# Rows kept on chip, plain stores instead of adding ones, and scatter-adds held back to the end of a graph-and-experts kernel

## The chip, the cores and the metric

One Trainium2 chip, of which the kernel uses one core. The metric is the device time in microseconds of one execution. Before the change it is 1616.14 us, the median of 3 runs (1612.79 to 1617.56).

## The reference, cut to what matters

There are 6250 nodes with 256 features. A graph layer comes first, then a feed-forward layer of 8 experts, of which each node uses its two best.

```python
x = x + _L0_gnn_ref(_layernorm(x), src, dst, W, b)      # 106250 edges, segment sums
x = x + _L0_ffn_ref(_layernorm(x)[None], Wr, br, ln_g, ln_b, W1, b1, W2, b2)[0]
# within _L0_ffn_ref, for each node (D = 256, H = 1024, E = 8, TOP_K = 2):
probs = softmax(xt @ Wr + br);  top_p, top_idx = top_k(probs, 2)
weights = top_p / top_p.sum(-1)
xe = xn[None] * ln_g[:, None] + ln_b[:, None]           # xn: layer norm of xt
h = gelu(einsum('end,edh->enh', xe, W1) + b1);  y = einsum('enh,ehd->end', h, W2) + b2
out = (weights[:, :, None] * sel).sum(axis=1)           # sel: y of the two chosen experts
```

So the output row of a node is its row after the graph layer (called its base row here) plus two weighted expert rows.

## The kernel before, in words

The nodes lie in 49 tiles of 128, one to a partition. `acc[:, t, :]` (called `row(t)`) holds tile t: first the sums of its edges' messages, then its base row, written by `hh` on VectorE (L1846). Tiles are taken in 10 chunks (`ENDS`); chunk 9 (`LAST`) is tiles 45 to 48. The edges' source rows are gathered by 768 indirect DMAs from GpSimd (`fetch`, L920) that run until 1288.7 us, with PE reducing them by matmuls. As soon as a chunk of tiles is complete, its nodes are normalised, routed (`r1` to `r9`) and scattered to the experts' areas in `xs` (step `xs`, L951, two DMAs a tile from GpSimd). Before the last chunk's scatter the unused places have to hold a blank row: eight stores from SP (`blanks`, L1124), for which the scatter waits (L949).

The experts work on blocks of 256 rows, the last eight (49 to 56) on blocks of 128: 57 in all. A block's rows and the two weight matrices are loaded (`ld`, `ld2`: L1150, L1157, L1165; the weights 1024 KB each, the rows 260 KB, the bias 128 KB), PE turns the rows (L1427), multiplies them up (L1443) and down (L1458), ACT and VectorE work between, and VectorE's `y` step (L1935) takes the result out of PSUM.

How results reach the output:
- Blocks 0 to 33 (chunks 0 to 7, tiles 0 to 40; `M0` = 34, `TG` = 41) are stored in `ys` by SP (`st`, L1113). After the last of these, tile t's two expert rows are fetched from `ys` by two indirect DMAs of GpSimd (step `cg`, L970) into a ring of 10 places (`NC`), and VectorE's step `cc` (L1948, L1949) weighs and sums them in `row(t)`.
- Blocks 34 to 56 are weighed on VectorE (`y`, L1941) and added to the rows of `out` in memory by scattering DMAs with an add (step `give`, L983): two for each of the blocks 34 to 48, one for each of 49 to 56, so 38 DMAs in 23 steps.
- The base rows of all tiles are written to `out` by SP (`nd2`, L1106) early on; therefore the sums of the tiles 0 to 40 are then *added* to `out` by four DMAs of GpSimd of 10, 10, 10 and 11 tiles (step `sums`, L992).

Two adding DMAs that touch the same row must not overlap. So the steps `give` and `sums` form one chain: each waits for the one before it to have landed (`wait_last`, L929). The first waits for the base stores. A block's `y` writes into a ring of 8 places (`NQ`), so `y` of block m waits for the `give` of block m - 8 (L1934), for blocks 45 to 56.

Each engine's instructions stand in one order that `plan()` writes beforehand, by its own costs and a simulated clock: `step_job` lets a `cg` go when GpSimd's clock is at most 2.5 us ahead and the last chunk has been sent (L376), gives it 2.5 us and counts its data there 2 us after (L429); `step_give` (L316) sends `sums` when its tiles' `cc` are placed, and `give` when its `y` is, with 5 us between any two. Steps of different kinds on one engine stand in the planned order, whatever comes late on the chip.

Of the kernel before, what the change touches and what calls it, by code (L numbers as in the profile page):

```python
# [74 lines left out]
NSUM = 4  # L75
# [76 lines left out]
def ends(g):  # L152

    c, a0, a1 = GROUPS[g]
    return c if a1 == CHUNKS[c][1] else None
# [33 lines left out]
def plan():  # L189

    order = []
    clock = {"PE": 0.0, "DVE": 0.0, "ACT": 0.0, "POOL": 0.0}
    s = {"now": 0.0, "bank": 0.0, "held": {}, "free": {}, "norms": -1, "nT": 0, "nW": 0, "hh": 0, "xr": 0, "placed": 0, "tabled": 0, "read": -1, "routed": -1, "loaded": 0, "asked": False, "given": 0, "base": 1e9, "late": 1e9, "summed": 0, "chain": 0.0,
         "pb": 0, "pe": 0, "pG": 0, "ps": 0, "pz": 0, "ph": 0, "po": 0, "pw": 0, "wj": 0, "zl": 0, "zat": 1e9}
    later, sent = [], {}

# [118 lines left out]

    def step_give():  # L316

        if max(s["chain"], s["base"]) > s["now"] or clock["POOL"] > s["now"] + 2.6 or LAST not in sent:
            return False
        if batches and batches[0][0] <= s["now"]:  # L320
            b = batches.popleft()[1]
            emit("sums", b, (("POOL", 1.3 * (SUMS[b][1] - SUMS[b][0])),), s["now"])
            s["summed"] += 1
        elif gives and (BLOCKS[gives[0]][0] < LAST or s["late"] <= s["now"]):
            emit("give", gives[0], (("POOL", 1.7 * GIVES[gives.popleft() - M0]),), s["now"])
            s["given"] += 1
        else:
            return False
        s["chain"] = clock["POOL"] + 5.0
        return True  # L330
# [32 lines left out]
    def step_job(front):  # L363
        while front and front[0].over():
            done = front.popleft()
            if done.chunk is not None:
                sends.append(Job(send_stages(done.chunk), done.at))
        for job in list(itertools.islice(front, 2 if front is jobs or front is sends else 1)):
            job.over()
            for chain in job.heads():  # L370
                if not chain.steps:
                    continue
                kind, arg, costs = chain.steps[0]
                if chain.at > s["now"] or not free(costs):
                    continue
                if kind == "cg" and (clock["POOL"] > s["now"] + 2.5 or LAST not in sent):  # L376
                    continue
                if kind in ("wa", "wc", "we", "nW", "lg", "r3") and s["bank"] > s["now"]:
                    continue
                if kind in PARTS and (PARTS[kind][0] in s["held"] or s["free"].get(PARTS[kind][0], 0.0) > s["now"]):  # L380
                    continue
                if kind in ("nT", "xT") and len(turns) >= 2 and turns[-2] not in used:
                    continue
                if kind == "hh" and s["norms"] < group_of(arg):
                    continue
                if kind == "r1" and arg != s["placed"] or kind == "r5" and arg != s["tabled"] or kind == "r6" and arg - 1 != s["routed"]:
                    continue
                if kind in ("nT", "nW", "xr") and arg != s[kind]:
                    continue
                if kind == "nd2" and s["hh"] < GROUPS[arg][2]:  # L390
                    continue
                if kind in AFTER_STEP and s[AFTER_STEP[kind]] < arg:
                    continue
                if kind == "lg" and s["read"] < group_of(arg) - 1:
                    continue
                if kind == "xr" and PREV[GROUPS[arg][0]] is not None and sent.get(PREV[GROUPS[arg][0]], 1e9) > s["now"]:
                    continue
                chain.steps.popleft()
                end = emit(kind, arg, costs, s["now"])
                if kind in PARTS:  # L400
                    s["held"][PARTS[kind][0]] = PARTS[kind][1]
                for part in [p for p, k in s["held"].items() if k == kind]:
                    del s["held"][part]
                    s["free"][part] = end
                if kind in ("nT", "xT"):
                    turns.append((kind, arg))
                if kind in ("nW", "lg"):
                    used.add(("nT" if kind == "nW" else "xT", arg))
                if kind in ("wb", "wd", "wf", "hh", "lr", "r5"):
                    s["bank"] = clock["DVE"]  # L410
                if kind == "nd1":
                    s["norms"] = arg
                if kind in ("nT", "nW", "hh", "xr", "wj", "pb", "pe", "pG", "ps", "pz", "ph", "po", "pw"):
                    s[kind] = arg + 1
                if kind == "r5":
                    s["placed"] = arg + 1
                if kind == "r6":
                    s["tabled"] = arg + 1
                if kind == "lr":
                    s["read"] = arg  # L420
                if kind == "cc" and any(arg == b1 - 1 for b0, b1 in SUMS):
                    batches.append((end, [b1 - 1 for b0, b1 in SUMS].index(arg)))
                if kind == "nd2" and ends(arg) in (LAST - 1, LAST):
                    s["base" if ends(arg) < LAST else "late"] = end + 4.0
                if kind == "sent":
                    sent[arg] = max(s["now"], clock["POOL"]) + 2.0
                if kind == "routed":
                    s["routed"] = arg
                chain.at = end + 2.0 if kind == "cg" else s["now"] + 4.0 if kind in ("pl", "pw", "blanks") else s["now"] if kind == "xs" else end  # L429
                job.at = max(job.at, end)  # L430
                return True
        return False
# [68 lines left out]
def gnn_ffn(nc, x, src, dst, W, b, Wr, br, ln_g, ln_b, W1, b1, W2, b2, out):  # L501
# [8 lines left out]
    with ctx:  # L510
# [183 lines left out]
        def row(t):  # L694
            return acc[:, t, 0:256]
# [70 lines left out]
        s_read7 = sem("s_read7")  # L766
        s_wr = sem("s_wr")
        s_stat = sem("s_stat")
        s_base = sem("s_base")
        s_out = sem("s_out")  # L770
        s_late = sem("s_late")
        s_xrow = sem("s_xrow")
# [27 lines left out]


        XS_BEFORE = [sum(2 * (t1 - t0) for t0, t1 in CHUNKS[:c]) for c in range(len(CHUNKS) + 1)]
        BASE_DMAS = sum(1 for c, a0, a1 in GROUPS if a0 < TG)
        OUT_DMAS = sum(1 for c, a0, a1 in GROUPS if a0 >= TG and c < LAST)
        LATE_DMAS = sum(1 for c, a0, a1 in GROUPS if c == LAST) + (1 if GROUPS[-1][2] - 1 > GROUPS[-1][1] else 0)
        NODE_T = {}
# [27 lines left out]
        def pool(e):  # L834
# [94 lines left out]
            def wait_last():  # L929

                if last is None:
                    e.wait_ge(s_base, 16 * BASE_DMAS)
                    e.wait_ge(s_out, 16 * OUT_DMAS)
                elif last[0] == "give":
                    e.wait_ge(s_give[last[1] % 2], given(last[1]))
                else:
                    e.wait_ge(s_sums[last[1]], 16)

            n_sent = 0
            last_row, last_node = e.to_reg(SPARE * BS - 1), e.to_reg(N - 1)  # L940
            for kind, arg in ORDER:
# [32 lines left out]
                elif kind == "give":  # L974
# [3 lines left out]
                    wait_last()  # L978
                    if BLOCKS[m][0] == LAST > BLOCKS[m - 1][0]:
                        e.wait_ge(s_late, 16 * LATE_DMAS)  # L980
                    last = ("give", a)
                    for i in range(size(m)):
                        e.indirect_dma_start(  # L983
                            out=out, out_offset=bass.IndirectOffsetOnAxis(ap=toks[:, a, i:i + 1].bitcast(u32), axis=0),
# [2 lines left out]
                elif kind == "sums":  # L987
                    b0, b1 = SUMS[arg]
                    e.wait_ge(s_comb, b1)
                    wait_last()  # L990
                    last = ("sums", arg)
                    e.dma_start(out=out[b0 * 128:b1 * 128, :].rearrange("(t p) c -> p t c", p=128), in_=acc[:, b0:b1, 0:256],  # L992
                                accum_op=ALU.add).then_inc(s_sums[arg], 16)
            for b in range(NSUM):
                e.wait_ge(s_sums[b], 16)
            for i in range(2):
# [2 lines left out]
        def sync(e):  # L999
# [54 lines left out]
            for kind, arg in ORDER:  # L1054
# [46 lines left out]
                elif kind == "nd2":  # L1101
                    c, a0, a1 = GROUPS[arg]
                    full = a1 if a1 < T else a1 - 1
                    e.wait_ge(s_stat, a1)
                    if full > a0:
                        e.dma_start(out[a0 * 128:full * 128, :].rearrange("(t p) c -> p t c", p=128),  # L1106
                                    acc[:, a0:full, 0:256]).then_inc(s_base if a0 < TG else s_out if c < LAST else s_late, 16)
                    if full < a1:
                        e.dma_start(out[48 * 128:N, :], acc[0:TAIL, T - 1, 0:256]).then_inc(s_late, 16)
                elif kind == "st":  # L1110
# [351 lines left out]
        def vector(e):  # L1462
# [269 lines left out]
            for kind, arg in ORDER:  # L1732
# [210 lines left out]
                elif kind == "cc":  # L1943
                    t = arg
                    e.wait_ge(s_cg[t % NC], 32 * (t // NC + 1))
                    if t == 0:
                        e.wait_ge(s_base, 16 * BASE_DMAS)
                    then(e.tensor_scalar(row(t), fetched_rows(t, 0), wts[:, 0, t:t + 1], None, ALU.mult))  # L1948
                    e.scalar_tensor_tensor(out=row(t), in0=fetched_rows(t, 1), scalar=wts[:, 1, t:t + 1], in1=row(t),  # L1949
                                           op0=ALU.mult, op1=ALU.add).then_inc(s_comb, 1)  # L1950

# [28 lines left out]
```

## Time and profile before

| what | value |
|---|---|
| median of 3 runs | 1616.14 us |
| profiled execution, its time | 1614.85 us |
| its span, first to last instruction | 1613.3 us |
| mean granted TensorE clock | 0.849 |
| busy: PE / VectorE / ScalarE / GpSimd | 72% / 63% / 40% / 72% |
| moved by DMA | 395.38 MB, 245 GB/s over the span |

The busy shares are means over stages with different limits, so that they don't tell what bounds one stage. GpSimd's share counts the time in which it makes a DMA's descriptors, not the time the data takes.

### The profile page before, as it was taken

Reading aid. Unit: us, or ns where it says so; the run is one execution under the profiler, and the core shown is the slowest. Engines: PE = TensorE matmul, PEld = TensorE weight load, DVE = VectorE, ACT = ScalarE, POOL = GpSimd, SP = SyncE. Lnnn points to the kernel's source line nnn. Section 1 sums busy time; section 2 is a strip of 40 time slices with the busy share of each in tenths; the row PEclk is TensorE's granted clock in tenths of the full one; section 3 lists DMA queues with packets and bytes.
Section 4 is the critical chain, followed back from the end, with each engine's and each line's share of the span. In section 5 each row is a group of like instructions: output and inputs, shape, how many; then the busy total and the mean of one; then the engine's idle time right before and its main releaser. Section 6 shows DMA issues by size and latency. Waiting matters only on the chain. (4 is left out here: it accounts for less than half of the span.)

```text
span 1613.3 us, 27172 instructions
## 1 busy us (share of the span) xinstructions
PE 1166.9 (72%) x9182; PEld 995.2 (62%) x9182; DVE 1023.7 (63%) x2809; ACT 644.5 (40%) x1273; POOL 1153.6 (72%) x1088
## 2 busy tenths in 40 slices
PE   6961756675661849879699696978949877899771
PEld 6961535463551738768578595856838665697661
DVE  8994757777683765847557475675746566666540
ACT  4964332124111424434245252424414353565550
POOL 8885777777777777777777777777777706786523
PEclk9999757666665979989899798988969998999996
DMA  8359878767757678777787777768668799999991
GB/s 255 114 177 340 295 257 274 255 208 246 236 190 249 193 247 276 233 258 251 224 289 249 254 251 251 245 222 264 218 208 264 241 280 270 264 324 295 308 304 21
DMA packets 271600, 395.38 MB, mean 245 GB/s; under 512 B 25205, under 2 KB 230935, under 8 KB 267365
## 3 DMA queue, kind: packets, MB, share of 16 engines
q1 hardware_dynamic: 205736, 244.70, 45.4%
q0 software_dynamic: 59360, 142.53, 29.8%
q10 hardware_dynamic: 6364, 6.40, 1.3%
q8 instruction: 74, 1.21, 0.3%
q14 instruction: 66, 0.53, 0.1%
HBM read 309.00 MB, written 85.67 MB: 245 GB/s over the span
## 5 line engine op out<-in xcount | busy, mean ns | idle before, releaser
L920 POOL DMA_INDIRECT gt<-zt,srcI x768 | 786.4, 1024 | 242.2 <-issue 177.9
L1325 PE MATMUL ps<-gt,S 128*128 128x257 f16 x1536 | 295.2, 317 | 172.1 <-DMA gt<-zt,srcI 161.6
L1443 PE MATMUL ps<-xe,w1b 128*128 128x256 f16 (+1 forms) x2736 | 336.3, 278 | 27.5 <-DVE xe L1901 16.9
L1272 ACT ACTIVATE h<-ps,cb 128x256 f32<-128x256 f32 (+1 forms) x456 | 224.5, 543 | 289.4 <-PE ps L1443 280.5
L1325 PEld LDWEIGHTS ps<-gt,S 128*128 128x128 f16 x1536 | 190.7, 151 | 231.6 <-DMA gt<-zt,srcI 207.0
L1458 PE MATMUL ps<-w2b,hT 128*128 128x256 f16 x2544 | 305.2, 278 | 16.8 <-DVE yb L1935 9.0
L1443 PEld LDWEIGHTS ps<-xe,w1b 128*128 128x128 f16 x2736 | 264.5, 103 | 70.4 <-DVE xe L1901 20.9
L1458 PEld LDWEIGHTS ps<-w2b,hT 128*128 128x128 f16 x2544 | 252.8, 100 | 52.5 <-issue 15.9
L1908 DVE SCALAR_TENSOR_TENSOR hT<-h,cb,hT 128x512 f16<-128x512 f32 (+1 forms) x228 | 161.3, 711 | 145.8 <-ACT hT L1276 145.2
L1276 ACT ACTIVATE hT<-h,cb 128x512 f16<-128x512 f32 (+1 forms) x228 | 157.8, 692 | 7.4
L951 POOL DMA_INDIRECT xs<-xrow,slI x98 | 100.8, 1029 | 77.2 <-DMA xs<-blank 47.6
L1235 ACT ACTIVATE aT<-ps 128x256 f32<-128x256 f32 x98 | 37.3, 380 | 256.7 <-PE ps L1388 256.5
L1776 DVE SCALAR_TENSOR_TENSOR acc<-ps,dhi,acc 128x257 f32 x208 | 91.0, 479 | 61.2 <-PE ps L1325 47.3
L880 POOL DMA_INDIRECT stg<-in_x,preI x64 | 103.9, 1624 | 19.6 <-issue 18.9
L1583 DVE TENSOR_TENSOR S<-dlo,S 128x1024 f16<-128x1024 f16 x104 | 71.1, 685 | 54.4 <-PE ps L1325 53.8
L983 POOL DMA_INDIRECT out<-gt,toks x32 | 51.7, 1615 | 73.9 <-DMA out<-gt,toks 30.9
L1259 ACT ACTIVATE xe<-ps 128x512 f16<-128x512 f32 (+1 forms) x57 | 31.4, 551 | 163.3 <-PE ps L1427 163.3
L1427 PE MATMUL ps<-ident,xb 128*128 128x128 f32 x212 | 37.8, 304 | 78.8 <-DMA xb<-xs 78.8
L1300 PE MATMUL ps<-ohh,ohl 128*128 128x49 bf16 x832 | 84.6, 278 | 9.3 <-DVE ohh L1536 8.7
L1300 PEld LDWEIGHTS ps<-ohh,ohl 128*128 128x128 bf16 x832 | 81.7, 150 | 12.4 <-DVE ohh L1536 12.4
L1368 PE MATMUL ps<-gb,w1b 128*128 128x1 f32 x256 | 48.4, 324 | 46.6 <-DMA w1b<-in_L_ffn_W 46.6
L1427 PEld LDWEIGHTS ps<-ident,xb 128*128 128x128 f32 x212 | 27.5, 156 | 82.9 <-DMA xb<-xs 82.4
(292 smaller groups left out, 1510.8 us busy)
## 6 DMA issues: line engine op xcount, KB each, us to landing
w1b<-ws SPq DMA_DIRECT2D x57, 1024.0 KB, 7.2
w2b<-ws SPq DMA_DIRECT2D x57, 1024.0 KB
ws<-w2b SPq DMA_DIRECT2D x16, 1024.0 KB, 5.2
xb<-xs SPq DMA_DIRECT2D x49, 260.0 KB, 7.6
gt<-zt,srcI POOLq DMA_INDIRECT x768, 4.7
ys<-yb SPq DMA_DIRECT2D x34, 256.0 KB, 5.0
zg<-zf SPq DMA_DIRECT2D x8, 1028.0 KB
gt<-zg SPq DMA_DIRECT2D x8, 1028.0 KB, 9.7
```

The costliest lines, as they stand in the source:

```text
L880: e.indirect_dma_start(out=stg[:, k % 2, c, :], out_offset=None, in_=x, in_offset=bass.IndirectOffsetOnAxis(ap=preI[:, c, k:k + 1].bitcast ...
L920: e.indirect_dma_start(out=gt[:, i % NG, :], out_offset=None, in_=zt, in_offset=bass.IndirectOffsetOnAxis(ap=srcI[:, c, r:r + 1].bitcast(u ...
L951: e.indirect_dma_start(out=xs, out_offset=bass.IndirectOffsetOnAxis(ap=slI[:, i, CHUNKS[c][0] + j:CHUNKS[c][0] + j + 1].bitcast(u32), axis=0),
L1272: inst = e.activation(h32[n % NH][:, z, 0:w], UP[n % 2][:, z * BS:z * BS + w], ACT.Gelu, bias=cb[m % 3][:, 2 * q + z:2 * q + z + 1], scale ...
L1276: e.activation(hT[m % 2][:, 0, 2 * q:2 * q + 2, 0:w], h32[n % NH][:, :, 0:w], ACT.Copy, scale=cb[m % 3][:, 9:10]).then_inc(s_hi, 1)
L1300: inst = e.matmul(PS[6][:, 0:T], ohl[c % 2][:, :, j], ohh[c % 2][:, :, j], start=(c == 0 and j == 0), stop=(c == NCH - 1 and j == TC - 1))
L1325: inst = e.matmul(PS[r % 2][:, 0:257], S[:, r % NS, :, c], gt[:, i % NG, part * 257:part * 257 + 257], start=(c == 0 and part == 0), stop= ...
L1443: inst = e.matmul(UP[n % 2][:, z * BS:z * BS + 128 * size(m)], w[:, l, kk, j * 128:(j + 1) * 128], xe[m % 2][:, k, kk, 0:128 * size(m)], s ...
L1458: inst = e.matmul(PY[:, h * D:(h + 1) * D], hT[m % 2][:, k, j, h * 128:(h + 1) * 128], w[:, l, j, :], start=(j == 0 and l == 0 and k == 0) ...
L1583: e.tensor_tensor(S[:, r % NS, :, :], dlo[:, r, :].unsqueeze(1).to_broadcast([128, 128, CT]), irun[:, :, :], ALU.is_equal).then_inc(s_S, 1)
L1776: inst = e.scalar_tensor_tensor(out=a, in0=PS[r % 2][:, 0:257], scalar=dhi[:, w, r:r + 1], in1=a, op0=ALU.mult, op1=ALU.add)
L1908: e.scalar_tensor_tensor(out=hT[m % 2][:, 1, 2 * q:2 * q + 2, 0:w], in0=h32[n % NH][:, :, 0:w], scalar=cb[m % 3][:, 9:10], in1=hT[m % 2][: ...
```

## The change: what it does

The base rows of the tiles 0 to 40 are no longer written to `out`; they stay in `row(t)`. Both instructions of `cc` now add into `row(t)` (before, the first overwrote it). The four `sums` DMAs are plain stores, wait for nothing but their tiles' `cc`, and leave the chain of adding DMAs. The first `give` waits for all four of them, and the planner places no `give` before they are placed. The `cg` steps of tiles 0 to 7 may stand ahead of the last chunk's scatter; those of the tiles 8 to 40 still stand behind it. No `cc` is placed before the last chunk's places are computed (`r5`). A fetch's data is counted there 4 us after it, not 2.

```diff
     def step_give():
-        if max(s["chain"], s["base"]) > s["now"] or clock["POOL"] > s["now"] + 2.6 or LAST not in sent:
+        if clock["POOL"] > s["now"] + 2.6:
             return False
         if batches and batches[0][0] <= s["now"]:
-            b = batches.popleft()[1]
-            emit("sums", b, (("POOL", 1.3 * (SUMS[b][1] - SUMS[b][0])),), s["now"])
+            emit("sums", batches.popleft()[1], (("POOL", 2.0),), s["now"])
             s["summed"] += 1
-        elif gives and (BLOCKS[gives[0]][0] < LAST or s["late"] <= s["now"]):
+        elif gives and s["summed"] == NSUM and s["chain"] <= s["now"] and (BLOCKS[gives[0]][0] < LAST or s["late"] <= s["now"]):
             emit("give", gives[0], (("POOL", 1.7 * GIVES[gives.popleft() - M0]),), s["now"])
...
-                if kind == "cg" and (clock["POOL"] > s["now"] + 2.5 or LAST not in sent):
+                if kind == "cg" and (clock["POOL"] > s["now"] + 2.5 or LAST not in sent and arg >= NC - 2):
+                    continue
+                if kind == "cc" and s["placed"] <= LAST:
                     continue
...
-                chain.at = end + 2.0 if kind == "cg" else ...
+                chain.at = end + 4.0 if kind == "cg" else ...
...
             def wait_last():
                 if last is None:
-                    e.wait_ge(s_base, 16 * BASE_DMAS)
                     e.wait_ge(s_out, 16 * OUT_DMAS)
-                elif last[0] == "give":
-                    e.wait_ge(s_give[last[1] % 2], given(last[1]))
+                    for b in range(NSUM):
+                        e.wait_ge(s_sums[b], 16)
                 else:
-                    e.wait_ge(s_sums[last[1]], 16)
+                    e.wait_ge(s_give[last % 2], given(last))
...
                 elif kind == "sums":
                     b0, b1 = SUMS[arg]
                     e.wait_ge(s_comb, b1)
-                    wait_last()
-                    last = ("sums", arg)
-                    e.dma_start(out=out[b0 * 128:b1 * 128, :].rearrange("(t p) c -> p t c", p=128), in_=acc[:, b0:b1, 0:256],
-                                accum_op=ALU.add).then_inc(s_sums[arg], 16)
+                    e.dma_start(out=out[b0 * 128:b1 * 128, :].rearrange("(t p) c -> p t c", p=128),
+                                in_=acc[:, b0:b1, 0:256]).then_inc(s_sums[arg], 16)
...
-                    if full > a0:
+                    if full > a0 >= TG:
                         e.dma_start(out[a0 * 128:full * 128, :].rearrange("(t p) c -> p t c", p=128),
...
                 elif kind == "cc":
-                    if t == 0:
-                        e.wait_ge(s_base, 16 * BASE_DMAS)
-                    then(e.tensor_scalar(row(t), fetched_rows(t, 0), wts[:, 0, t:t + 1], None, ALU.mult))
+                    then(e.scalar_tensor_tensor(out=row(t), in0=fetched_rows(t, 0), scalar=wts[:, 0, t:t + 1], in1=row(t),
+                                                op0=ALU.mult, op1=ALU.add))
```

## Rows read from the trace of the kernel before

**Rows 1.** The page: busy time (share of the span) and instructions of each engine.
```profile
PE 1166.9 (72%) x9182; PEld 995.2 (62%) x9182; DVE 1023.7 (63%) x2809; ACT 644.5 (40%) x1273; POOL 1153.6 (72%) x1088
```

**Rows 2.** Busy time by stretch; the last three columns: granted clock, DMA share, GB/s.
```profile
1318.00:1336.00 18.00, 16.14 (x153) 14.13 (x152) 15.36 (x67) 13.70 (x24) 0.00 (x0) 1.00 1.06 316
1346.00:1400.00 54.00, 37.80 (x310) 31.50 (x308) 29.64 (x87) 23.77 (x43) 43.10 (x37) 0.87 0.88 260
1400.00:1462.00 62.00, 61.24 (x547) 54.29 (x545) 39.58 (x96) 37.90 (x69) 42.23 (x37) 0.97 1.09 305
...
1548.00:1576.00 28.00, 23.71 (x282) 20.99 (x280) 13.43 (x43) 20.61 (x51) 9.71 (x6) 0.96 0.99 311
```

**Rows 3.** Timeline of GpSimd, 1290 us to the end: start, duration; idle before, releaser.
```profile
1336.30 1.02 POOL L951 DMA_INDIRECT xs<-xrow,slI  x1 [47.62 <-DMA xs<-blank]
...
1346.67 1.61 POOL L983 DMA_INDIRECT out<-yb,toks  x1 [0.30 <-issue]
...
1515.37 0.99 POOL L970 DMA_INDIRECT S<-ys,cidx  x1 [0.32 <-issue]
...
1529.05 2.00 POOL L992 DMA_DIRECT2D out<-acc  x1 [6.50 <-DMA out<-gt,toks]
1548.55 1.66 POOL L983 DMA_INDIRECT out<-gt,toks  x1 [17.50 <-DMA out<-acc]
...
1558.00 1.55 POOL L983 DMA_INDIRECT out<-gt,toks  x1 [5.92 <-DMA out<-gt,toks]
...
1568.54 1.79 POOL L983 DMA_INDIRECT out<-gt,toks  x1 [7.11 <-DMA out<-gt,toks]
...
1576.56 1.56 POOL L983 DMA_INDIRECT out<-gt,toks  x1 [4.37 <-DMA out<-gt,toks]
...
1605.84 1.56 POOL L983 DMA_INDIRECT out<-gt,toks  x1 [2.57 <-issue]
```

**Rows 4.** Timeline of SP's queue: the last store to `ys`, the last blank store.
```profile
1305.74 0.54 SPq L1113 DMA_DIRECT2D ys<-yb  x1
...
1328.21 0.38 SPq L1124 DMA_DIRECT2D xs<-blank  x1
```

**Rows 5.** Landing of the 34 stores to `ys` (L1113).
```profile
DMA to landing us min/median/max: 2.7/5.0/11.5
```

**Rows 6.** The fetches (L970): who waited for them, their landing, GpSimd's time by group.
```profile
  DVE acc L1948: 39.6, 20
...
DMA to landing us min/median/max: 2.8/5.9/10.3
...
L970 POOL DMA_INDIRECT S<-ys,cidx x34 | 34.3, 1010 | 10.4 <-issue 10.1 <-DVE acc L1949 0.3
```

**Rows 7.** The four adding DMAs `sums` (L992): landing; and a plain store of the page.
```profile
DMA to landing us min/median/max: 12.4/14.1/18.7
...
ws<-w2b SPq DMA_DIRECT2D x16, 1024.0 KB, 5.2
```

**Rows 8.** Landing of single scatter-adds: those issued at 1358.38 and at 1498.47 us.
```profile
out<-yb,toks POOLq DMA_INDIRECT x1, 4.4
...
out<-gt,toks POOLq DMA_INDIRECT x1, 7.5
```

**Rows 9.** Timeline of VectorE: `cc` of tile 0; `y` of blocks 41, 42, 48, 56.
```profile
1357.40 0.35 DVE L1948 TENSOR_SCALAR acc<-S,wts 128x256 f32<-128x256 f32 x1 [5.16 <-DMA S<-ys,cidx]
1357.79 0.48 DVE L1949 SCALAR_TENSOR_TENSOR acc<-S,wts,acc 128x256 f32<-128x256 f32 x1
...
1431.67 0.75 DVE L1935 SCALAR_TENSOR_TENSOR gt<-ps,cb,b2b 128x512 f32<-128x512 f32 x1
...
1442.58 0.75 DVE L1935 SCALAR_TENSOR_TENSOR gt<-ps,cb,b2b 128x512 f32<-128x512 f32 x1
...
1517.50 0.75 DVE L1935 SCALAR_TENSOR_TENSOR gt<-ps,cb,b2b 128x512 f32<-128x512 f32 x1
...
1579.46 0.48 DVE L1935 SCALAR_TENSOR_TENSOR gt<-ps,cb,b2b 128x256 f32<-128x256 f32 x1 [2.06 <-PE ps L1458]
```

More of the change, by code:

```diff
@@ L192, in plan @@
     clock = {"PE": 0.0, "DVE": 0.0, "ACT": 0.0, "POOL": 0.0}
-    s = {"now": 0.0, "bank": 0.0, "held": {}, "free": {}, "norms": -1, "nT": 0, "nW": 0, "hh": 0, "xr": 0, "placed": 0, "tabled": 0, "read": -1, "routed": -1, "loaded": 0, "asked": False, "given": 0, "base": 1e9, "late": 1e9, "summed": 0, "chain": 0.0,
+    s = {"now": 0.0, "bank": 0.0, "held": {}, "free": {}, "norms": -1, "nT": 0, "nW": 0, "hh": 0, "xr": 0, "placed": 0, "tabled": 0, "read": -1, "routed": -1, "loaded": 0, "asked": False, "given": 0, "late": 1e9, "summed": 0, "chain": 0.0,
          "pb": 0, "pe": 0, "pG": 0, "ps": 0, "pz": 0, "ph": 0, "po": 0, "pw": 0, "wj": 0, "zl": 0, "zat": 1e9}
@@ L422, in step_job @@
                     batches.append((end, [b1 - 1 for b0, b1 in SUMS].index(arg)))
-                if kind == "nd2" and ends(arg) in (LAST - 1, LAST):
-                    s["base" if ends(arg) < LAST else "late"] = end + 4.0
+                if kind == "nd2" and ends(arg) == LAST:
+                    s["late"] = end + 4.0
                 if kind == "sent":
@@ L428, in step_job @@
                     s["routed"] = arg
-                chain.at = end + 2.0 if kind == "cg" else s["now"] + 4.0 if kind in ("pl", "pw", "blanks") else s["now"] if kind == "xs" else end
+                chain.at = end + 4.0 if kind == "cg" else s["now"] + 4.0 if kind in ("pl", "pw", "blanks") else s["now"] if kind == "xs" else end
                 job.at = max(job.at, end)
@@ L768, in gnn_ffn @@
         s_stat = sem("s_stat")
-        s_base = sem("s_base")
         s_out = sem("s_out")
@@ L802, in gnn_ffn @@
         XS_BEFORE = [sum(2 * (t1 - t0) for t0, t1 in CHUNKS[:c]) for c in range(len(CHUNKS) + 1)]
-        BASE_DMAS = sum(1 for c, a0, a1 in GROUPS if a0 < TG)
         OUT_DMAS = sum(1 for c, a0, a1 in GROUPS if a0 >= TG and c < LAST)
@@ L980, in pool @@
                         e.wait_ge(s_late, 16 * LATE_DMAS)
-                    last = ("give", a)
+                    last = a
                     for i in range(size(m)):
@@ L1104, in sync @@
                     e.wait_ge(s_stat, a1)
-                    if full > a0:
+                    if full > a0 >= TG:
                         e.dma_start(out[a0 * 128:full * 128, :].rearrange("(t p) c -> p t c", p=128),
-                                    acc[:, a0:full, 0:256]).then_inc(s_base if a0 < TG else s_out if c < LAST else s_late, 16)
+                                    acc[:, a0:full, 0:256]).then_inc(s_out if c < LAST else s_late, 16)
                     if full < a1:
```

## The prediction, made before the changed kernel was run

> **What bounds the kernel now.** I read the page's shares first [rows 1]: no engine is busy for three quarters of the span, so the bound changes by stage. The change acts where the results reach the output, after the gathers; so next came the table by stretches from there on, then the timelines of GpSimd and VectorE.
>
> Up to 1288.7 us GpSimd issues the gathers one after another. The planner treats everything up to the last store to `ys` as before, since none of the edited conditions is met before it; so I count this stage unchanged. Then GpSimd idles 47.62 us until the last blank store has landed, and starts the last scatters at 1336.30 [rows 3]. From 1346.67 it issues adds, fetches and sums, the last fetch at 1515.37. PE is full only from 1400 to 1462 (61.24 of 62 us) and the DMA engines are full too, share 1.09 at 305 GB/s; before that PE lost 16 of 54 us [rows 2], partly because VectorE stood before `cc` steps whose rows had not landed, 39.6 us in 20 waits [rows 6], the first of 5.16 us [rows 9].
>
> The end: the last `y` starts at 1579.46 [rows 9], the last scatter-add at 1605.84, the span ends at 1613.3. After the fourth `sums` (issued 1529.05) the chain runs without a break: 17.5 us for that DMA, then steps of 9.45, 10.54 and 8.02 us (starts 1548.55, 1558.00, 1568.54, 1576.56), then the eight single ones of blocks 49 to 56, 36.7 us from 1576.56 to the end of the span [rows 3]. So GpSimd's chain of landings sets the end, and the experts' last blocks run just ahead of it.
>
> **Part by part.**
>
> *Eight fetches ahead of the scatters.* Tile 0's fetch waits for the last store to `ys`, issued at 1305.74 [rows 4], landing in 5.0 us, 11.5 at most [rows 5]: so from 1311 to 1317. It has the last scatters queued behind it. Sixteen DMAs at 1.01 us plus 0.30 between them [rows 6, 3] are 21 us: done at 1332 to 1338, where the scatters start at 1336.30. Price 0 to 2 us. They also move 2.1 MB while the blanks are under way, in a stretch with the DMA full (1.06) [rows 2]; at its 316 GB/s that is 6.6 us, part of which falls in the slack before 1318. The last blank was issued only at 1328.21 [rows 4]. Together 0 to 8 us; I take 3. What they save is 21 us of GpSimd later.
>
> *Adds leave the fetching stage.* From the end of the scatters (1346.67 + 3 = 1349.7) GpSimd has 66 fetches at 1.30 us, 85.8 us, and three `sums` at 2.2 us (2.0 as at 1529.05, and 0.2 to 0.3 between), 6.6 us: 1442.1. The last fetch starts about 1440.8. It lands in 5.9 us at the median, 10.3 at most [rows 6]; with the DMA as full as in 1400 to 1462 I take 6.6: 1447.4. Then its `cc`, and VectorE's lag: 3.6 us, so 1451.
>
> That lag is the uncertain piece. A `cc` grows by 0.13 us (0.35 to 0.48 for its first instruction [rows 9]), 5.3 us over 41 tiles, beside PE as long as VectorE has room. In the fetching stage it takes about four tiles a block where it took about three: VectorE's 39.58 us of 62 [rows 2] rises by some 1 us a tile, to about 48 of 62. So it fits, but `cc` and the experts' steps stand in one order, and a wait before one delays the other. Bounds: 1447 (no lag) to 1470 (half of the 39.6 us of waits comes again). Against it: the eight early tiles have landed, and the planner leaves 2 us more for the others.
>
> *Plain sums.* The fourth is the one in the way: the first `give` waits for it, with all others queued behind on GpSimd. As an add such a DMA took 12.4 to 18.7 us; 1 MB stored plainly took 5.2 us [rows 7], times 1.375 for the size 7.2. Between these ends I take 10, nearer the plain store, since the DMA is still full when it starts. So the chain of adds begins at S = 1461, range 1450 to 1485.
>
> The Trainium skill ("DMA: Bandwidth & Descriptors", section "Anatomy of one DMA — SWDGE (gpsimd) path") gives an estimate for a DMA issued here: 2.0 us plus its bytes at 436 GB/s. For 1.44 MB that is 5.3 us, and the sum would come out 4.7 us lower. The trace's adding DMAs took more than twice that [rows 7], so it doesn't bear the rule out where the queues are full.
>
> *All adds after it.* Before, 12 of the 15 double steps had gone before the fourth `sums`, with landings hidden behind fetches. Now all 23 stand in one row with nothing between. A double step costs 1.9 us to the second issue, its landing, and 0.7 us until the next issue (an estimate: the last single step stood 2.57 us idle between its predecessor's issue and its own [rows 3]). Landings: 4.4 us at 262 GB/s, 7.5 us in the full stretch [rows 8]; so 7.0 to 10.1, and 8.0 to 10.5 measured in the chain [rows 3]. Nothing below is excluded: with a nearly idle DMA it may be 6. The first four fall while the experts wait for them (`y` of block 45 needs the fourth) and fetches are over: 4 x 7.2 = 28.8. Five fall beside full blocks, where the loads (2 x 1024 + 260 + 128 KB) come to 228 GB/s: 5 x 7.6 = 38.0. Six fall beside the half blocks, which load as much in less time: 6 x 9.3 = 55.8, the mean of the three measured. Together 122.6: the single steps start at 1583.6, where they started at 1576.56. Then 36.7 us as before: span 1620.3.
>
> *Is PE late too?* `y` of block 45 comes at S + 28.8 + 1 = 1491. Three full blocks at 10.92 us (1431.67 to 1442.58 for one [rows 9]) and 62 us for the eight half blocks (1517.50 to 1579.46 [rows 9]) give the last `y` at 1586, level with the chain. Its stops after 1500 may shrink, since the fourth `sums` no longer collides with them, which only brings it below the chain. This ring makes PE's end follow the adds, whatever PE gains between 1346 and 1400.
>
> *SP's stores.* Fourteen stores go, 5.4 MB of the 395.38, nearly all beside the gathers, which GpSimd's own issuing paces: 0. If the bytes were the bound there it would be 5.4 MB at the page's 245 GB/s, 22 us; GpSimd is busy or between two issues nearly all of that stage, so I leave that end out of the sum. SP's wait for the statistics stays.
>
> The profiled execution took 1.55 us more than its span, and stands 1.3 us below the median: 1620.3 + 1.55 = 1621.9, so 1622 against 1616.14. The first adding step moved later by more than 100 us, and what was hidden under fetches is now paid in the open; that eats the 21 us moved forward and the gain on the sums.
>
> **Rivals.**
>
> *Landings are light (faster).* If VectorE doesn't lag and the fourth store takes 7 us, S is 1452; if nine of the double steps land in 4.4 us or less (7.0 each) and six take 8.0, they need 111: singles from 1563, PE's stops gone and its last `y` at 1572 or so. The end is 1599.7 + 1.55, with up to 6 more where single steps share the DMA with the last half blocks: 1601 to 1607, say 1605. For it: 4.4 us at 262 GB/s [rows 8], and the total of DMA work falls. Against it: three measured chain steps of 8.0 to 10.5. It wins where the 15 steps take under 8 us on average.
>
> *VectorE's order binds (slower).* In the fetching stage every `cc` waits for rows, every wait holds up the experts' splits, so PE, and so the next `cc`. Each of the first three `sums` sits in the same queue as the fetches behind it and delays them. At 18 us of lag and a fourth store of 14 us S is 1479.4 (14.4 and 4 more than above) and the time 1640. It decides from a lag of 8 us. For it: 39.6 us of such waits [rows 6]. Against it: the ring of 10 and the doubled allowance.
>
> *It doesn't move the end.* The eight fetches start late and push the scatters by what they save, and the chain, one landing after another, ends where it did: 1616.
>
> **How the numbers follow.** Forecast 0.50, own range 1611 to 1633. Light landings 0.27, VectorE's order 0.15, no move 0.08. A difference of 0.3%, 4.8 us, is about what can be told from none, so the borders are 1611.3 and 1621.0. The forecast lies 0.07 below, 0.18 between, 0.25 above. Faster 0.07 + 0.27 = 0.34; same 0.18 + 0.08 = 0.26; slower 0.25 + 0.15 = 0.40. A tenth at either end leaves 1602 to 1640.
>
> **What would show it.** GpSimd's idle before the first scatter falls from 47.6 us to under 10, with 16 fetches ahead, and that scatter starts by 1340. No scatter-add before the last fetch, near 1441. A wait of 7 to 14 us before the first scatter-add, at 1461 or so. Double steps 7 to 10 us apart, `y` of block 45 freed by the fourth, the single steps starting near 1584. It is wrong if the chain starts before 1450 or its 15 steps take under 112 us (then faster), if the last `y` instead of the chain sets the end, or if the first scatter starts after 1345.

## The result, and the profile after

The changed kernel takes 1637.25 us, the median of 4 runs (1627.73 to 1639.37), against 1616.85 us of the kernel before in the same comparison. The ratio is 1.0123, 95% interval 1.0101 to 1.0145: slower by 1.2%. The prediction was 1622, range 1602 to 1640, with "slower" the likeliest of the three signs; the measured time lies 2.75 us below the upper end. The profiled execution took 1636.55 us with a span of 1635.1. Ratios below are to the kernel before, run in the same comparison, and leave out disturbed runs (over 1.5% above the fastest of their kernel), which the medians still hold.

The page's first part of the changed kernel answers to [rows 1]; the line under it is its HBM line.
```profile
PE 1174.2 (72%) x9182; PEld 996.0 (61%) x9182; DVE 1026.0 (63%) x2809; ACT 644.4 (39%) x1273; POOL 1152.5 (70%) x1088
...
HBM read 309.00 MB, written 80.29 MB: 238 GB/s over the span
```
The engines' work is the same, and 5.4 MB of writes are gone. No engine's busy time tells where 20 us went. GpSimd's timeline does; this is the changed kernel's, answering to [rows 3] (start, duration, idle before, releaser; L968 is a fetch, L988 a store of sums, L981 a scatter-add).
```profile
1317.25 0.95 POOL L968 DMA_INDIRECT S<-ys,cidx  x1 [25.36 <-DMA ys<-yb]
...
1344.27 1.02 POOL L949 DMA_INDIRECT xs<-xrow,slI  x1 [6.02 <-DMA xs<-blank]
...
1444.74 0.96 POOL L968 DMA_INDIRECT S<-ys,cidx  x1 [0.30 <-issue]
1453.30 1.12 POOL L988 DMA_DIRECT2D out<-acc  x1 [7.60 <-DVE acc L1944]
1462.39 1.63 POOL L981 DMA_INDIRECT out<-yb,toks  x1 [7.96 <-DMA out<-acc]
...
1492.54 1.55 POOL L981 DMA_INDIRECT out<-gt,toks  x1 [5.51 <-DMA out<-yb,toks]
...
1498.95 1.55 POOL L981 DMA_INDIRECT out<-gt,toks  x1 [2.99 <-issue]
...
1505.98 1.55 POOL L981 DMA_INDIRECT out<-gt,toks  x1 [3.48 <-issue]
...
1546.14 1.67 POOL L981 DMA_INDIRECT out<-gt,toks  x1 [6.51 <-DMA out<-gt,toks]
...
1556.92 1.67 POOL L981 DMA_INDIRECT out<-gt,toks  x1 [7.25 <-DMA out<-gt,toks]
...
1596.90 1.67 POOL L981 DMA_INDIRECT out<-gt,toks  x1 [1.92 <-DMA out<-gt,toks]
...
1625.74 1.55 POOL L981 DMA_INDIRECT out<-gt,toks  x1 [1.90 <-DMA out<-gt,toks]
```
The reader is to see three stretches. The fetches end 71 us sooner than before (1444.74; 1515.37 in [rows 3]). The chain of adds starts at 1462.39, where it started at 1346.67. From there every wait between two steps that the profile gives a cause ends with a landing: 15 double steps take 134.5 us (1462.39 to 1596.90) and the single ones with the last landing 38.2.

VectorE's `y` of the blocks 44, 45 and 56 in the changed kernel (answering to [rows 9]): the ring binds, and block 45 waits 10.11 us for an add to land.
```profile
1477.16 0.75 DVE L1931 SCALAR_TENSOR_TENSOR gt<-ps,cb,b2b 128x512 f32<-128x512 f32 x1
...
1498.27 0.75 DVE L1931 SCALAR_TENSOR_TENSOR gt<-ps,cb,b2b 128x512 f32<-128x512 f32 x1 [10.11 <-DMA out<-gt,toks]
...
1596.27 0.48 DVE L1931 SCALAR_TENSOR_TENSOR gt<-ps,cb,b2b 128x256 f32<-128x256 f32 x1 [4.06 <-DMA out<-gt,toks]
```

Who waited for whom in the changed kernel between 1340 and 1600 us (total us, times, longest):
```profile
POOL out L981 <- DMA out<-gt,toks: 55.9, 10, 7.5
...
DVE gt L1931 <- DMA out<-gt,toks: 39.6, 8, 10.1
PE ps L1454 <- DVE gt L1931: 20.2, 6, 9.3
```
Two more rows of the changed kernel: how long VectorE waited for the rows of fetches (L968), answering to [rows 6], and the landing of the four stores of sums (L988), answering to [rows 7]:
```profile
  DVE acc L1942: 21.6, 14
...
DMA to landing us min/median/max: 8.2/9.7/10.7
```

### The profile page after: what moved, and what is told of

Read it like the earlier page. It is cut to its first block and busy times, and to the rows that moved or that the text cites. A ratio compares the mean times of both kernels' runs of the same rounds, so it can differ in the third digit from the quotient of the medians.

```text
span 1635.1 us, 27167 instructions
## 1 busy us (share of the span) xinstructions
PE 1174.2 (72%) x9182; PEld 996.0 (61%) x9182; DVE 1026.0 (63%) x2809; ACT 644.4 (39%) x1273; POOL 1152.5 (70%) x1088
## 5 line engine op out<-in xcount | busy, mean ns | idle before, releaser
L1321 PE MATMUL ps<-gt,S 128*128 128x257 f16 x1536 | 299.0, 319 | 179.0 <-DMA gt<-zt,srcI 171.0
L1454 PE MATMUL ps<-w2b,hT 128*128 128x256 f16 x2544 | 310.8, 281 | 25.1 <-DVE gt L1931 20.2
L981 POOL DMA_INDIRECT out<-gt,toks x32 | 50.9, 1591 | 89.4 <-DMA out<-gt,toks 73.7
L1364 PEld LDWEIGHTS ps<-gb,w1b 128*128 128x128 f32 x256 | 49.0, 298 | 46.7 <-issue 46.6
```

The source lines that it names most:

```text
L1321: inst = e.matmul(PS[r % 2][:, 0:257], S[:, r % NS, :, c], gt[:, i % NG, part * 257:part * 257 + 257], start=(c == 0 and part == 0), stop= ...
L1364: inst = e.matmul(PV[:, j:j + 1], w3[:, kk, j * 128:(j + 1) * 128], gb[:, ex, 2 + kk:3 + kk], start=(kk == 0), stop=(kk == 1))
L1454: inst = e.matmul(PY[:, h * D:(h + 1) * D], hT[m % 2][:, k, j, h * 128:(h + 1) * 128], w[:, l, j, :], start=(j == 0 and l == 0 and k == 0) ...
```

## The experiments

**One: where the early fetches stand.**

```diff
-  if kind == "cg" and (... or LAST not in sent and arg >= NC - 2):
+  if kind == "cg" and (... or LAST not in sent):
```

> The changed kernel, with the eight early fetches put back behind the last chunk's scatters; all else as changed. Theory (the 23 adding steps stand in one chain behind the last fetch and the last store, and end 173 us after it): the scatters start some 5 us earlier, but 82 instead of 66 fetches stand before the fourth store, 21 us more, so the chain starts about 15 us later and the time is about 1650 (1643 to 1656). Rival (the early fetches delay the scatters and cost as much as they save): within 5 us of the changed kernel, 1633 to 1641, or under it.

Measured: 1645.12 us, ratio 1.0189 (1.0162 to 1.0217), as the theory had it. The early fetches gain 8 us in the changed kernel. The last scatters start at 1340.28 instead of 1344.27, the chain at 1477.67 instead of 1462.39. These 15.3 us are what was expected, but only half reached the end: the 15 double steps took 125.5 us (1477.67 to 1603.18), not 134.5. A later chain has more of its steps in the lull in which the experts already wait for it: here four of them took 6.3 to 7.1 us, in the changed kernel two.

**Two: the early fetches alone, in the kernel before.**

```diff
-  if kind == "cg" and (clock["POOL"] > s["now"] + 2.5 or LAST not in sent):
+  if kind == "cg" and (clock["POOL"] > s["now"] + 2.5 or LAST not in sent and arg >= NC - 2):
+      continue
+  if kind == "cc" and s["placed"] <= LAST:
       continue
```

> The kernel before, with only this of the change: eight tiles' fetches may stand ahead of the last scatters and no weighing step stands before the last chunk's places. Theory: GpSimd ends its fetches some 15 us earlier, but the fourth adding sum then stands before six double adding steps instead of three, so most is given back: 1606 to 1620, 1613. Rival (the early fetches load the DMA beside the blank stores and delay the last scatters by 8 us, and that is what made the change slow): 1622 to 1630.

Measured: 1614.48 us, ratio 0.9988 (0.9974 to 1.0003): no difference. The fourth sum is issued at 1507.94, where it was 1529.05, but six double steps stand behind it instead of three. In the timeline of this kernel (L994 the fourth sum, L985 adds), the first and the last of the six, the first single step and the last:
```profile
1507.94 2.02 POOL L994 DMA_DIRECT2D out<-acc  x1 [9.08 <-issue]
1522.12 1.66 POOL L985 DMA_INDIRECT out<-gt,toks  x1 [12.16 <-DMA out<-acc]
...
1570.82 1.57 POOL L985 DMA_INDIRECT out<-gt,toks  x1 [6.29 <-DMA out<-gt,toks]
...
1576.18 1.56 POOL L985 DMA_INDIRECT out<-gt,toks  x1 [1.93 <-DMA out<-gt,toks]
...
1604.40 1.56 POOL L985 DMA_INDIRECT out<-gt,toks  x1 [1.89 <-DMA out<-gt,toks]
```
The single steps start at 1576.18, in the kernel before at 1576.56 [rows 3]. Twenty microseconds of GpSimd's issuing bought nothing at the end.

**Three: holding back alone.**

```diff
-  elif gives and (BLOCKS[gives[0]][0] < LAST or s["late"] <= s["now"]):
+  elif gives and s["summed"] == NSUM and (BLOCKS[gives[0]][0] < LAST or s["late"] <= s["now"]):
```

> The kernel before, with only this of the change: no scatter-add is placed before all four sums. They stay adding DMAs, base rows are still stored early. Theory (holding back is what costs): fetches end about 1453 and the fourth sum, an add of about 18 us, lands about 1487; 15 double steps of 9 us and 38 us of single ones follow: 1655 to 1668, 1660. Rival (holding back costs nothing, something else in the change does): 1610 to 1622.

Measured: 1672.15 us, ratio 1.034 (1.030 to 1.0381): holding the adds back costs 58 us by itself, more than expected. Of the profiled executions, this one's gathers ended 8 us later than the kernel before's, and from their end to the last instruction it took 51 us more (376.0 against 324.6). The chain starts at 1511.38 instead of 1487. From there one landing after another paces it, as in the other kernels with held adds. The fourth sum, the first two double steps, and the first and the last single step:
```profile
1493.37 2.05 POOL L992 DMA_DIRECT2D out<-acc  x1 [11.51 <-DVE acc L1949]
1511.38 1.67 POOL L983 DMA_INDIRECT out<-yb,toks  x1 [15.96 <-DMA out<-acc]
1517.88 1.56 POOL L983 DMA_INDIRECT out<-yb,toks  x1 [2.97 <-DMA out<-yb,toks]
...
1635.31 1.59 POOL L983 DMA_INDIRECT out<-gt,toks  x1 [2.01 <-DMA out<-gt,toks]
...
1663.76 1.56 POOL L983 DMA_INDIRECT out<-gt,toks  x1 [1.89 <-DMA out<-gt,toks]
```
Its first step, in the lull, takes 6.50 us. The other parts of the change together (plain sums that wait for no add, the base rows kept, the planner's other conditions and 4 us allowed for a fetch) take 27 of the 58 us back (1672.15 to 1645.12 of experiment one), the early fetches 8 more (to 1637.25).

**Four: two chains instead of one.**

```diff
-  else:
-      e.wait_ge(s_give[last % 2], given(last))
+  elif last:
+      e.wait_ge(s_give[(last - 1) % 2], given(last - 1))
...
-  out=out, ...
+  out=(out, out2)[a % 2], ...
```

> The changed kernel, with the adding steps of every second block directed at a scratch copy of the output, so that each waits only for the one before the last (the odd blocks' additions are thus left out of the output; all DMAs and bytes stay). Theory: the single chain of landings is the bound, two landings now overlap, the ring frees blocks 45 to 56 in time, and what ends is the experts' last block near 1580 and a few adds: 1590 to 1605, 1597. Rival (DMA load or the experts bound the end, not the chain): over 1625.

Measured: 1582.84 us, ratio 0.9801 (0.9775 to 0.9827), 54 us under the changed kernel and 7 under the range expected, with the same DMAs, bytes and blocks. The chain starts where it did (1462.65). Its last adds wait for the experts (`DVE gt`), not for landings, and the last `y` starts at 1570.16:
```profile
1462.65 1.68 POOL L982 DMA_INDIRECT out<-yb,toks  x1 [11.20 <-DMA out<-acc]
...
1561.03 1.55 POOL L982 DMA_INDIRECT out<-gt,toks  x1 [5.50 <-DVE gt L1938]
1567.86 1.55 POOL L982 DMA_INDIRECT out<-gt,toks  x1 [5.28 <-DVE gt L1938]
1571.31 1.55 POOL L982 DMA_INDIRECT out<-gt,toks  x1 [1.90 <-DVE gt L1938]
```
So the single chain is the bound, not the experts and not the bytes as such. With the experts as the bound the kernel ends near 1580.

**Five: what a landing shares the DMA with.** This and the rest fell on two other chips. On the second chip (experiments five to eight) the kernel before took 1843.09 us, on the third (the repeats of five and eight, nine and ten) 1839.34 us: 14% more, mostly in the gathers, which ended at 1454.9 to 1487.5 us in the profiled executions there and at 1288.0 to 1296.5 on the first chip. I don't explain this; times are compared within one chip only, and the gathers' end has to be looked at beside them.

```diff
+  few = 2 if m >= 44 else 8
-  e.dma_start(w1b[m % 2]...rearrange("p (q c) -> p q c", q=8), ws[0][bass.ds(ex, 1), :, :, :]...)
+  e.dma_start(w1b[m % 2]...rearrange("p (q c) -> p q c", q=8)[:, 0:few, :], ws[0][bass.ds(ex, 1), 0:few, :, :]...)
```
and the same for `w2b`.

> The changed kernel, with only a quarter of each weight matrix loaded for the blocks 44 to 56 (the rest of the tile keeps older weights, so these blocks' values are not the reference's; every instruction and semaphore stays). Theory: a double adding step lasts 9 us on average because its landing shares the DMA with the weight loads; without most of them it lasts about 6.5 to 7, as the four in the lull did, so the 15 take about 100 instead of 134 us and the time falls by 30: 1600 to 1612, 1606. Rival (the landing is a fixed latency of an adding scatter, whatever else moves): 15 steps still near 134 us, 1632 to 1640.

> The changed kernel with a quarter of each weight matrix loaded for the blocks 44 to 56 (these blocks' values are left wrong), once more, since the first comparison fell on a chip on which all kernels, the one before too, took 14% longer. There its 15 double steps took 108.5 us against 134.9 us of a kernel with full loads. Theory: the same here, 15 steps in 100 to 110 us and the time some 25 to 30 us under the changed kernel's 1637: 1605 to 1613. Rival (fixed latency of the adding scatter): 134 us and 1632 to 1640.

Measured: 1858.01 us, ratio 1.0071 (1.0032 to 1.0109), on the second chip, and 1849.56 us, ratio 1.0063 (1.0026 to 1.0101), on the third. The absolute times can't be held against those expected. On the second chip experiment six, with full loads, took 1882.27 us, 24 more; it differs in the cuts of its stores too. The length of the chain can be compared. With full loads its 15 double steps took 134.9 us on the second chip (experiment six, 1704.77 to 1839.69) and 134.5 on the first. With quarter loads they took 108.5 us on the second chip and 109.1 on the third (1698.96 to 1808.04), more than the 100 first expected. The two kernels over these stretches, full loads, then quarter ones (length; PE, PE loads, VectorE, ACT, GpSimd; clock, DMA share, GB/s):
```profile
1704.00:1840.00 136.00, 112.36 (x1117) 96.86 (x1115) 57.65 (x167) 76.91 (x167) 48.28 (x31) 0.94 0.85 242
```
```profile
1699.00:1808.00 109.00, 101.02 (x1088) 90.02 (x1085) 57.24 (x164) 74.03 (x162) 47.75 (x30) 1.00 0.59 122
```
So 26 us of the 134 go with three quarters of the weight loads: a landing is no fixed latency. The other 7.2 us a step stay. Of the waits between these steps the profile puts one down to the experts (3.3 us for `DVE gt`) and the others to landings or to nothing that it can name, but PE is busy 101 of 109 us: the experts are hardly faster than the chain here.

**Six: a small last store.**

```diff
-SUMS = [(TG * i // NSUM, TG * (i + 1) // NSUM) for i in range(NSUM)]
+SUMS = [(0, 13), (13, 26), (26, 38), (38, 41)]
```

> The changed kernel, with the four plain stores cut into 13, 13, 12 and 3 tiles instead of 10, 10, 10 and 11. Theory: the chain's start sets the end one to one; the last store lands in 4 to 7 us instead of 9, so the chain starts 3 us earlier: 1631 to 1637, 1634. Rival (the third store, of 12 tiles, is then the late one, or the start doesn't matter): no difference, 1637.

Measured, on the second chip: 1882.27 us, ratio 1.0207 (1.0131 to 1.0284). The changed kernel with even cuts didn't run there, so the 3 us can't be told. The chain starts 6.8 us after the fourth store's issue (1697.98 to 1704.77), where it was 9.1. But what ended GpSimd's idle time there was, by the profile, VectorE and no store, and the third store had itself waited 21.6 us for its tiles. Inconclusive.

**Seven: the same cut in the kernel before with the early fetches.**

> The kernel before with the eight early fetches, and its four adding sums cut into 13, 13, 12 and 3 tiles. Theory: the last sum lands 8 us sooner but the others take longer in the same chain, and their bytes are the same; what counts is the total of landings in the chain: 1606 to 1616, 1611. Rival (only the last sum's landing is in the open): 1602 to 1606.

Measured, second chip: 1846.19 us, ratio 1.0028 (0.9999 to 1.0058), against 0.9988 with even cuts on the first. No gain over the kernel before. In its trace the fourth sum, issued at 1736.99, first waits 13.54 us for the third to land; that a shorter last sum is paid for by a longer one ahead of it fits this, but the even cuts didn't run on this chip, so it is not shown.

**Eight: sums aside.** The kernel before, its order kept, with the sums stored plainly into a scratch copy and no part of the chain:

```diff
-  wait_last()
-  last = ("sums", arg)
-  e.dma_start(out=out[b0 * 128:...], in_=acc[...], accum_op=ALU.add)...
+  e.dma_start(out=out2[b0 * 128:...], in_=acc[...])...
```

> The kernel before in its order, with the four sums stored plainly into a scratch copy of the output and out of the chain of adds (so the output leaves out the sums of the tiles 0 to 40; the adds need not be held back). Theory: the chain of landings is the bound from 1346 us to the end already in the kernel before, and the four sums fill some 60 us of it; without them the adds keep up with the experts and the end follows the last block: 1578 to 1592, 1585. So the change bought these 60 us and paid them, and more, with the 115 us in which no add runs. Rival (the sums are hidden behind fetches, except the fourth): 1595 to 1603.

> The kernel before in its order with the four sums as plain stores into a scratch copy, out of the chain (their sums are left out of the output), once more on another chip. Theory (the four sums fill much of the chain of landings of the kernel before): 1578 to 1592. Rival (only the fourth sum is in the open): 1595 to 1603.

Measured: 1842.43 us, ratio 0.9993 (0.9954 to 1.0032), on the second chip, and 1839.85 us, ratio 1.0012 (0.9969 to 1.0055), on the third: nothing. Both expectations missed. The timeline of the second of the two suggests why: the sums wait for their `cc` in GpSimd's queue, with the adds behind them, 20.87 us the third and 28.95 us the fourth.
```profile
1708.34 1.02 POOL L991 DMA_DIRECT2D out<-acc  x1 [20.87 <-DVE acc L1947]
...
1767.79 1.15 POOL L991 DMA_DIRECT2D out<-acc  x1 [28.95 <-DVE acc L1947]
```
So without the landings the same queue waits for VectorE. The kernel before has no trace from these chips to hold against this, and how much the four sums weigh on the first chip stays open.

**Nine and ten: a fuller chain.** Both are the kernel before with the early fetches. Nine lets adds stand before the last chunk is sent; ten also puts adds ahead of sums and allows 2 us, not 5, between steps:

```diff
-  if max(s["chain"], s["base"]) > s["now"] or clock["POOL"] > s["now"] + 2.6 or LAST not in sent:
+  if max(s["chain"], s["base"]) > s["now"] or clock["POOL"] > s["now"] + 2.6:
...                                       # ten only:
-  if batches and batches[0][0] <= s["now"]:
+  if batches and batches[0][0] <= s["now"] and not (gives and s["summed"] < NSUM - 1 and gives[0] < NB - 8):
...
-  s["chain"] = clock["POOL"] + 5.0
+  s["chain"] = clock["POOL"] + 2.0
```

> The kernel before with the eight early fetches, and with adds allowed in the planned order before the last chunk is sent, so that block 34's stands ahead of the last scatters. Theory (the chain is full from about 1400 us on, not before it): one step moved out of 27 gains little, since seven double steps and the fourth sum still stand behind the last fetch: 1608 to 1618. Rival (every step moved forward gains its 9 us): 1600 to 1606.

> The same, and the planner prefers adds to sums and leaves 2 instead of 5 us between steps of the chain, so that only one double step stays behind the fourth sum where six did. Theory (the end is the chain's total of landings plus the time in which it is empty): the chain is kept busy through the fetches, the single steps start right after the last blocks, 1590 to 1602, 1597, faster than both kernels. Rival (a fuller chain delays the fetches, so the fourth sum and the rest come later): 1612 to 1625.

Measured, third chip: nine 1820.23 us, ratio 0.9912 (0.9875 to 0.9949); ten 1821.25 us, the median of 1801.68, 1812.12, 1830.39 and 1923.61, ratio 0.984 (0.9765 to 0.9915), which rests on the first two of these. Both beat the kernel before there. Carried over by its ratio to the first chip, nine would take some 1600 to 1603 us, the rival's range and not the theory's, and ten some 1588 to 1591, at the lower end of the theory's range and far from its rival's.

That nine gains by its early add is not shown. In the profiled executions its gathers ended at 1454.9 us and those of experiment eight's second run, on the same chip, at 1472.6: 17.7 of the 30.8 us between their spans lie ahead of anything the edit touches on GpSimd, whose order is the same up to there. From the gathers' end on, nine took 352.8 us, experiment eight's second run 365.9 and experiment seven, on the second chip, 357.2. The early fetches alone, nine without its add, didn't run on the third chip, nor did the changed kernel.

## Why the prediction was right, and the term that was off

*The stage before.* Counted as unchanged; the gathers ended at 1291.9 instead of 1288.7. That is within what executions differ by: in experiment three, where nothing ahead of it is changed, they ended at 1296.5 (1344.76 less 48.23 idle).

*Eight fetches ahead.* Tile 0's fetch started at 1317.25 (1311 to 1317 given), the sixteen took 21 us as worked out, and the scatters started at 1344.27, where 1339.3 was taken and 1345 was the limit. So the sign "by 1340" failed. The gathers' end counts for 3 of these 8 us. The rest is the fetches' price: from the gathers' end to the first scatter it took 47.6, 47.7 and 48.2 us in the three traces of the first chip without early fetches (before, experiments one and three) and 52.2 to 53.1 in the three with them (changed, two and four), so 5 us, where 3 was taken. The scatters still waited 6.02 us for the blank stores: the fetches did not hold GpSimd but delayed the blanks.

*The fetching stage.* 66 fetches and three stores took 90.5 us, 92.4 predicted. An issue of a plain store costs GpSimd 1.02 us, not the 2.0 of an adding one. The fourth store was issued at 1453.30 (1451) and landed in time for 1462.39: 9.1 us where 10 was taken. S was 1461 predicted, 1462.39 measured. VectorE's waits for rows fell from 39.6 to 21.6 us.

*The page's formula.* The Trainium skill ("DMA: Bandwidth & Descriptors", "Anatomy of one DMA — SWDGE (gpsimd) path") would give an estimate of 5.3 us for the fourth store; it landed in 8.2 us, the four in 8.2 to 10.7. The measurement decides: here, with the DMA engines 93% busy over 1400 to 1462 us and 81% over its last 12, the formula is too low.

*The 15 double steps: the mis-sized term.* 122.6 us predicted, 134.5 measured, 11.9 of the 14.8 us by which the span exceeded the forecast (1635.1 against 1620.3; the other 2.9 are 1.4 of S and 1.5 of the tail). The changed kernel over the first three steps, the next two, the seven after them and the last three (columns as above):
```profile
1462.39:1492.54 30.15, 27.48 (x252) 24.47 (x250) 13.72 (x33) 20.43 (x37) 9.43 (x7) 1.00 0.92 268
1492.54:1505.98 13.44, 6.82 (x41) 5.15 (x42) 2.76 (x6) 0.26 (x1) 6.35 (x5) 0.62 0.52 92
1505.98:1578.07 72.09, 58.82 (x654) 51.00 (x651) 30.65 (x95) 47.25 (x111) 22.44 (x15) 0.94 0.96 281
1578.07:1596.90 18.83, 13.28 (x120) 10.56 (x120) 8.28 (x30) 4.93 (x12) 9.58 (x6) 0.86 0.48 110
```
The prediction had four short steps at once, which "fall while the experts wait for them". The experts didn't yet wait: in the first three steps PE was busy 27.5 of 30.2 us and the DMA share 0.92, and they took 11.15, 10.07 and 8.93 us; only two fell in the lull, 6.41 and 7.03. And beside full blocks I took 7.6 us, where 9.90 and 10.63 were measured (9.7 to 11.0 over the seven steps from 1505.98 to 1578.07). The landings had been set by the GB/s beside them: with 4.4 us "at 262 GB/s", full blocks at 228 GB/s looked light. That was misread. 262 GB/s is the mean of 1340 to 1400 us; in the 7.6 us after the issue of that add the kernel before moved 136 GB/s at a DMA share of 0.63 (columns as in [rows 2]):
```profile
1358.40:1366.00 7.60, 2.86 (x14) 2.10 (x15) 5.45 (x15) 0.59 (x1) 6.38 (x5) 0.50 0.63 136
```
The 7.5 us of [rows 8] was the right one: with it a double step is 10.1 us by the prediction's own sum. The last three, as the loads ran out, took 6.42, 6.97 and 5.44. Experiment five shows that the weight loads make the difference.

*PE.* The last `y` was forecast at 1586 and started at 1596.27, 4.06 us of it waiting for an add. PE's end followed the chain, as said. Experiment four shows the experts with the chain out of their way: last `y` at 1570.16.

*Rivals.* Light landings needed under 8 us a step; it was 9.0. That VectorE's order binds gave 1640, the nearest number, but by a chain that starts at 1479.4, and it started at 1462.39 with VectorE's waits for rows nearly halved: near by number only. That the change doesn't move the end is false by 1.2%. The forecast's mechanism, landings formerly hidden under fetches now in the open, is shown by experiments three (holding back alone: 58 us) and four (the same work with two chains: 54 us less). Its size was not: 1637.25 lies outside the forecast's own range of 1611 to 1633, and the range as a whole took it in only because it reached up to that rival's 1640.

## What to carry to other kernels

When writes have to follow one another by a completed landing, count the chain as an engine of its own: its busy time is steps times landing, under the load that will be there, and most of its idle time before the first step is lost (8 of 15 us in experiment one, 37 of 49 in three). A change that frees an engine but starts such a chain later has to be priced by the chain. Moving an engine's work forward pays only if the order then puts the chain's steps into the room.

## What the runs showed that was not expected

- The chain's length was the same on two chips, 134.5 and 134.9 us for the 15 steps with full loads, while the kernel before took 14% longer on the second.
- A later chain is shorter (134.5, 125.5 and 123.9 us for starts at 1462, 1478 and 1511), since the experts wait for it and their loads stop (over the first six steps of the latest, experiment three's, the DMA share was 0.48 and PE was busy 16 of 42 us): 49 us of later start cost 37 us at the end.
- GpSimd issued a plain store of 1280 KB in 1.02 us, an adding one in 1.85 to 2.01; with one of 1408 KB in each group, landings were 8.2 to 10.7 against 12.4 to 18.7 us [rows 7].
